# Block stores split over two DMA queues, a rotated order of the attention passes, and earlier slot preparation in a fused attention and mixture kernel

## What is computed

```python
q = x @ Wq + bq; k = x @ Wk + bk; v = x @ Wv + bv        # x layer-normed
k = k / jnp.maximum(jnp.linalg.norm(k, axis=-1, keepdims=True), 1e-12)
alpha, beta, gate = sigmoid(x @ Wa + ba), sigmoid(x @ Wb + bb), sigmoid(x @ Wg + bg)
def step(S, ins):
    trans = a_t[:, :, None] * (I - b_t[:, :, None] * kkT)
    S = jnp.einsum('bij,bjk->bik', S, trans) + b_t[:, :, None] * vkT
    return S, jnp.einsum('bc,bcd->bd', q_t, S) * g_t
x = x + (o @ Wo + bo)                                    # then, layer-normed again:
logits = jnp.einsum('bsd,etd->bset', xn, se)             # xn, se: RMS-normed x and slots
slots = jnp.einsum('bsd,bset->betd', xn, softmax(logits, axis=1))
processed = gelu(slots @ w1) @ w2
out = jnp.einsum('bnd,bsn->bsd', processed, softmax(logits over all slots))
x = x + out
```

## Time and profile before

| | us |
|---|---|
| median of 3 runs | 1261.44 |
| lowest and highest of them | 1257.5, 1261.8 |
| the profiled execution | 1255.7 |
| its span | 1254.0 |

### The profile page before, as it was taken

The page is one execution under the profiler, slowest core; times in us unless marked ns, Lnnn a source line. Parts: engine busy times, 40 slices in busy tenths (PEclk is TensorE's granted clock), DMA queues, the critical chain, the costliest instruction groups (busy, mean ns, idle before and its releaser), DMA issues.

```text
span 1254.0 us, 26991 instructions
## 1 busy us (share of the span) xinstructions
PE 1138.2 (91%) x8600; PEld 862.8 (69%) x8600; DVE 949.4 (76%) x2195; ACT 737.6 (59%) x1385; POOL 299.9 (24%) x373
## 2 busy tenths in 40 slices
PE   3588989898888977999999999999999999999998
PEld 2377767676677766568678568678468688477687
DVE  4568878788788884899757798656898666998655
ACT  3445555555555542578755478755477854487754
POOL 3345544555555541100002000002000012000012
PEclk9689999999999997999999999999999999999999
DMA  5112332223223313331327121337030346000045
GB/s 181 36 36 71 92 93 69 68 68 76 69 69 90 88 53 89 102 91 32 84 53 165 37 43 27 84 67 160 27 68 5 80 88 144 22 1 1 18 103 132
DMA packets 176941, 90.33 MB, mean 72 GB/s; under 512 B 117152, under 2 KB 170400, under 8 KB 176864
## 3 DMA queue, kind: packets, MB, share of 16 engines
q1 hardware_dynamic: 169808, 71.74, 24.5%
q0 software_dynamic: 5792, 17.05, 4.9%
q10 hardware_dynamic: 1264, 0.53, 0.2%
HBM read 38.42 MB, written 25.69 MB: 51 GB/s over the span
## 4 chain that ended last, share of the span: by engine, by line
PE 42%; DVE 23%; issue 10%; DMA 9%; ACT 6%; SPq 5%; DVEq 0%; POOL 0%; ACTq 0%; POOLq 0%
PE m_wide L1952 14%; DMA Mrep<-M_dram 8%; PE m_wide L1835 7%; PE m_wide L1929 5%; SPq L285 5%; PE m_wide L1915 4%; DVE m_Dm L1534 3%; DVE tmp L569 2%; PE m_wide L1940 2%; DVE Zc L580 2%; DVE m_El L1542 2%; DVE cmax L1505 2%; DVE rmax L1511 2%; ACT m_Eh L1717 2%; PE m_wide L1889 2%
## 5 line engine op out<-in xcount | busy, mean ns | idle before, releaser
L1472 POOL DMA_DIRECT2D out_dram<-m_o x64 | 35.5, 555 | 639.6 <-DVE m_o L1656 636.5
L1889 PE MATMUL m_wide<-m_X,m_Eh 128*128 128x257 f16 (+1 forms) x1024 | 171.1, 273 | 2.3 <-DVE m_El L1542 2.2
L1952 PE MATMUL m_wide<-m_Ph,m_Th 128*128 128x257 f16 x512 | 141.7, 277 | 10.5 <-DVE m_Pl L1581 10.5
L1835 PE MATMUL m_wide<-seT,XT 128*128 128x512 f16 x672 | 147.3, 379 | 0.1
L1952 PE MATMUL m_wide<-m_Ph,m_Tl 128*128 128x257 f16 x512 | 140.7, 275 | 0.0
L1952 PE MATMUL m_wide<-m_Pl,m_Th 128*128 128x257 f16 x512 | 140.4, 274 | 0.0
L1889 PE MATMUL m_wide<-m_X,m_El 128*128 128x257 f16 (+1 forms) x512 | 139.7, 273 | 0.0
L1835 PEld LDWEIGHTS m_wide<-seT,XT 128*128 (+1 forms) x672 | 65.5, 98 | 77.6 <-ACT L L1690 1.1
L1889 PEld LDWEIGHTS m_wide<-m_X,m_Eh 128*128 128x128 f16 x1024 | 99.2, 98 | 19.6 <-issue 3.5
L1690 ACT COPY L<-m_wide 128x512 f32<-128x512 f32 (+1 forms) x112 | 65.2, 585 | 77.0 <-PE m_wide L1835 76.2
L1753 ACT COPY m_Tl<-m_wide 128x1024 f16<-128x1024 f16 x64 | 64.7, 1011 | 75.5 <-PE m_wide L1940 75.5
(11 more groups left out here) (197 smaller groups left out, 2723.2 us busy)
## 6 DMA issues: line engine op xcount, KB each, us to landing
L<-in_L_attn_x_dram SPq DMA_DIRECT2D x16, 512.0 KB, 7.3
Mrep<-M_dram SPq DMA_DIRECT2D x16, 512.0 KB
x_dram<-x SPq DMA_DIRECT2D x16, 512.0 KB, 7.2
m_X<-X_dram SPq DMA_DIRECT2D x128, 64.0 KB, 1.8
m_x1t<-x_dram POOLq DMA_DIRECT2D x32, 256.0 KB, 3.5
out_dram<-m_o POOLq DMA_DIRECT2D x64, 128.0 KB, 2.5
X_dram<-Xh SPq DMA_DIRECT2D x16, 256.0 KB, 2.3
X_dram<-Xl SPq DMA_DIRECT2D x16, 256.0 KB, 2.3
```

The costliest lines, as they stand in the source:

```text
L1835: last = pe.matmul(lg[t % 4], XT[:, sx * KD + k, bass.ds((4 * g + t) * P, P)], seT[:, ss, k, z * HS:(z + 1) * HS], start=(c == 0), stop=(c ...
L1889: last = pe.matmul(acc[v][q], e[t % 4][:, qs], X[:, sx, bass.ds(4 * g + t, 1), 0:XW].rearrange("q a n -> q (a n)"), start=first and e is E ...
L1952: last = pe.matmul(co[p], a, pp[:, e, 0:XW], start=(c == 0), stop=(c == 3 * NS - 1))
```

## The change

What it does, in the attention:

- SP stores 4 of the 8 blocks (`range(NBK // 2)`), ACT the other 4, from its own queue, in a new `blocks_out` between `products(i+2, 0)` and `normalise(i+4)`.
- The read back is two DMAs, rows 0 to 7 of each block and then rows 8 to 15, each with a semaphore of its own. The base starts after the first; `product` 8 waits for the second.
- The border between two passes is moved on PE, ACT and DVE: `products` 2, `doubling` 2, `updates` and most `keys_values` now stand at the head of the next pass. On DVE `doubling` 2 comes after the first pair of the base, the first `biases` come before it, the others after pairs 6 and 7, `low_part` comes after all of `statistics`, and `moments` after `right_side`. On ACT `turned_x` 1 comes after `turned_Z` 1, `normalised` after `key_norms`, and `decayed` before `updates`. On POOL both `cut`, `residual` and the decayed queries change place.
- The slots are scaled and split in pass -1 instead of passes 12 and 13, turned on PE in pass 13 instead of 14, and the first four `early_logits` are made in pass 14. SP's first transposed load of X moves from pass 14 to pass 13.

In the mixture: `tp_ps` starts at 2 instead of 1, and ACT's waits on it are raised by one, so that only DVE's wait in `split_weights` is looser. ACT makes one tile of `weights` ahead of the first `processed_high` instead of two. The semaphore `going` is joined with `turning`.

```diff
             def blocks_out(c, q):
                 sp.wait_ge(M_ok, c + 1)
-                for e in range(NBK):
+                for e in range(NBK // 2):
...
-                sp.dma_start(Mrep[:, :, :, :].rearrange("p s b t -> p (s b t)"),
-                             M_dram.rearrange("e (a s) b t -> e a (s b t)", a=1).broadcast_to([NBK, BS, BS * B * BS]))\
-                    .then_inc(Mrep_in, 16)
+                for rows_in, s in ((Mrep_in, 0), (Mrep_late, HROWS)):
+                    sp.dma_start(Mrep[:, s:s + HROWS, :, :].rearrange("p s b t -> p (s b t)"),
+                                 M_dram[:, s:s + HROWS].rearrange("e (a s) b t -> e a (s b t)", a=1)
+                                 .broadcast_to([NBK, BS, HROWS * B * BS])).then_inc(rows_in, 16)
...
                     dve.wait_ge(col_ok, s)
+                    if s == HROWS:
+                        dve.wait_ge(Mrep_late, 16 * (c + 1))
...
+            def blocks_out(c, q):
+                act.wait_ge(M_ok, c + 1)
+                for e in range(NBK // 2, NBK):
+                    act.dma_start(M_dram[e],
+                                  M[q][e * BS:(e + 1) * BS, :, e * BS:(e + 1) * BS]).then_inc(M_out, 16)
...
                 def low_turned(k, t):
                     p, n = t % 2, b * HB + 2 * k + t // 2 + 1
-                    act.wait_ge(tp_ps[p], n + 1)
+                    act.wait_ge(tp_ps[p], n + 2)
...
-                for t in range(2):
-                    weights(0, t)
+                weights(0, 0)
                 for q in range(QS):
                     processed_high(0, q)
-                    if q < 2:
-                        weights(0, q + 2)
-                    elif q == 2:
+                    if q < QS - 1:
+                        weights(0, q + 1)
+                    if q == 2:
                         act.activation(table[:, 1:2], zero[:, :], ACT.Gelu)
...
-                pe.sem_inc(tp_ps[p], 1)
+                pe.sem_inc(tp_ps[p], 2)
```

More of the change, by code:

```diff
@@ L355, in step @@
                     store_x1(i)
+                if isinstance(i, int) and i == NCH - 3:
+                    blocks_landed(i + 2)
+                    sp.wait_ge(slots_ok, 1)
+                    load_XT0(0, XT0_PARTS[0])
                 if live(i + 4) and live(i + 2):
@@ L769, in step @@
                     next_state(i + 1, r, 3)
+                if live(i + 3):
+                    decays_from_start(i + 3, r, 0)
+                if live(i + 1):
+                    residual(i + 1, r)
+                if live(i + 2):
+                    doubling(i + 2, q, 0)
+                if live(i + 1):
+                    statistics(i + 1, 0)
+                if live(i + 3):
+                    decays_from_start(i + 3, r, 1)
+                if at == -2:
+                    mixture_weights(5)
+                if at == -1:
+                    slots_low()
+                if live(i + 4):
+                    turned_low(i + 4, 1)
+                if live(i + 1):
+                    statistics(i + 1, 1)
                 if at == NCH - 1:
@@ L958, in step @@
                 at = i if isinstance(i, int) else None
-                if at == NCH - 1:
-                    for t in range(4):
-                        early_logits_out(t)
-                if live(i):
-                    normalised(i)
+                if live(i + 1):
+                    turned_Z(i + 1, 2)
+                if live(i + 1):
+                    products(i + 1, 2)
+                if at == NCH - 2:
+                    turned_slots((6, 7))
+                if live(i + 1):
+                    turned_state(i + 1)
+                if live(i + 2) and live(i + 3):
+                    decayed(i + 2, q)
                 if live(i + 1):
@@ L973, in step @@
                     decay_and_step(i + 3, r)
+                if at == NCH - 1:
+                    for t in range(4, 8):
+                        early_logits_out(t)
+                if live(i):
+                    normalised(i)
+                if at == NCH - 2:
+                    early_logits_out(1)
+                    early_logits_out(2)
                 if live(i + 3):
                     queries(i + 3, r)
-                if live(i + 2) and live(i + 3):
-                    decayed(i + 2, q)
                 if live(i + 3):
@@ L1018, in _ @@
             steps(act, step)
-            for t in range(4, NT):
+            for t in range(8, NT):
                 early_logits_out(t)
@@ L1291, in _ @@
             steps(pe, step)
-            for t in range(NT):
+            for t in range(4, NT):
                 early_logits(t)
```

211 lines of the change are left out of this document (111 added, 100 removed).

## The result

The changed kernel takes 1263.22 us (median of 20 runs, 1257.26 to 1272.06), the kernel before 1257.41 (20 runs, 1246.76 to 1264.17). The ratio is 1.0052, 95% interval 1.0028 to 1.0076: slower by about half a percent, which is the border that the prediction drew. The profiled execution took 1258.68 us, 4.5 less than the median of its kernel; its span is 1256.9 against 1254.0 before.

A forecast was written before the change was run, and what follows sets the result against it. A ring of waits, no full engine, bounds the attention; PE nearly bounds the mixture. Terms +20, +1, -6.5, -9.8 make +4.7, rounded to +4: 1259.7 us profiled, 1265.5 median; 8-in-10 range 1249 to 1285.

The forecast's parts named there:

- The step from the profiled execution to the median: Profiled execution 1255.7 us against a median of 1261.44: 5.7 us difference, carried over to the changed kernel unchanged.
- The bounds of the half read: Attention, read back of the blocks' first half: 4.6 us expected, between 3.4 (bytes over all engines) and 5.6 (half the gain lost).
- The ring: Attention, chain of waits from one M to the next: 29.5 us per pass against 27.85, +20 us over 12 passes.
- The likeliest case: The forecast itself: half read holds up the base until +15.4, a pass of 29.5 us, 1265.5 us; chance 0.49.
- The start: Start of the attention, casts and slot work moved there: +1 us, with -2 and +4 as ends.
- the cover given to the slot work at the start: Attention's start: casts arrive before chunk 0's base, where DVE waited anyway; 3.25 us scaling and 1.7 us casting precede the next.
- The tail: End of the attention, slot work leaving the path: last three passes 6.5 us shorter, with -3 and -10 as ends.
- The mixture: Mixture, looser DVE wait 1.6 us and reordered `weights` 0.8 us per batch: -9.8 us, ends -6 and -11.
- The read is early enough: Attention: half read lands within 3.4 us, DVE itself bounds the base; pass of 28.2 us, 1250 in all; chance 0.22.
- Later still: Attention: `low_part` keeps 2.10 us as POOL runs late, half read takes 5.6; +23 us, 1288; chance 0.17.
- The two queues share the issue: Attention: ACT's four stores take 5 us, `normalise` and all behind start 2.5 us later; +30 us, 1296; chance 0.04.
- The mixture does not gain: Mixture: waits only change name, ACT's exponentials or last outputs come as late; +10 against the forecast, 1275; chance 0.08.

## Why the prediction was right in the end, and where it was not

The predicted 1265.5 us stand against 1263.22. That closeness is luck in good part: two terms were off by some 6.5 us each, with opposite signs. The step from the profiled execution to the median was off as well. I carried over 5.7 us, from three runs of the kernel before; its median of 20 runs is 1257.41, only 1.7 above the profiled execution, and for the changed kernel the step is 4.5. So the medians differ by 5.8 us where the forecast had 4. Two slips in the sum are small: 22.7 and 6.9 make 29.6 and not 29.5 us (1.2 us over 12 passes), and four times 2.4 is 9.6 and not 9.8. The bounds of the half read do not follow from their words either: a quarter of 5.6 us above 1.8 gives 3.2, and half of the gain lost gives 6.0, where 3.4 and 5.6 stand.

**The ring, mechanism right, size too large.** The likeliest case was what happened. Its steps against the means of the twelve passes: `low_part` done at +10.2 (9.8 measured), read issued at +10.8 (10.8), first half 4.6 us (4.6), base at +15.4 (15.4), updates at +16.3 (16.3). Only the last two terms were mis-sized: from the updates to the heads 6.4 us, taken from before, took 5.9 in 11 of 12 passes (6.0 in the mean), and from there to M 6.7 instead of 6.9. That makes the 0.5 us per pass between 29.5 and 28.98. The steps are right as means, but not in each pass: in five of the twelve PE's clock fell behind the pause at `turn_x`, the DVE work behind it came later, and DVE waited for the read only 0.0, 0.2, 0.6, 0.9 and 1.5 us there, against 1.2 to 1.7 in the others. I had priced that pause at its length alone, and its clock only as a part of a rival. Part of it returns in other executions: the profile of the version with DVE's wait of the mixture put back has the same attention code and a ring of 29.79, because PE's clock fell there between the updates and the heads in 6 of 12 passes, against 1. The median of the changed kernel, 4.5 us above its profiled execution, fits that, but I have no trace of a median run.

**The start, wrong.** I counted +1 with +4 as the upper end; it was +7.6. The step that failed is the cover given to the slot work at the start, "arrive later in front of the base of chunk 0 where DVE waited anyway" and the 3.25 and 1.7 us ahead of the next base. I counted them as work against a wait of DVE, and did not follow that in the new order `doubling` 2, and so the updates, stand behind them. Against before M(2) - M(1) grew by 4.6 us (35.2 from 30.6), and with the slots late it was 28.6. The second piece is ACT's stores: M(1) - M(0) is 31.8 us with them, 29.6 before, and 27.9 in the version with all stores on SP, since PE's `turn_x` of the next chunk, which waits for `normalise`, starts 4.8 us behind M(0) with them and 0.9 in that version. This holds for the rotated order only: in the order of before the split made this stretch shorter, 26.5 us. The third stays open: M(0) is 1.8 us later (30.25 from 28.45). It lies at 27.6 to 28.5 in four profiles of the old order and at 30.2 to 31.9 in nine of the rotated one, but at 28.1 in a tenth, so whether the order or the first loads make it I can't tell. M(3) - M(2) is 1.0 us shorter, and with that the pieces make the 7.6.

**The tail, right within 1 us.** -5.5 against -6.5. What ends last there are DVE's maxima, 1.2 us per tile, one behind the other in both profiles but for one `low_part`: from the first early one to the mixture's first it is 21.3 us before and 20.6 after. So 4.9 of the 5.5 us are won ahead of them. That the four early logits gained nothing by themselves fits this, but no run tests it. The slot work is tested: with it back in pass 12, the way from M of chunk 15 to the first early maximum grows by 2.5 and 3.5 us.

**The mixture, right, a little too small.** -12.8 against -9.8, and outside its end of -11: DVE's wait was worth 2.1 us per batch instead of 1.6, the order of the exponentials, by subtraction, 1.1 to 1.3 instead of 0.8. PE's wait ahead of `combine` fell as said, to about 1 us per batch:

```profile
PE m_wide L2006 <- DVE m_Pl L1636: 4.2, 4, 1.1
```

**The rivals.** "The read is early enough" did not happen: DVE waited in 11 of the 12 passes. "Later still" neither: POOL was idle and `low_part` took 1.21 us; but its other half, PE's clock falling in the pauses at `turn_x`, did happen in five of the twelve passes, and these take 28.5 to 30.0 us. "The two queues share the issue" is refuted: four stores take 2.54 us on SP and 2.5 to 2.9 on ACT, side by side, against 5.07 and 5.14 for eight on one in the rows shown. "The mixture does not gain" is refuted by both runs on it.

**What I had not seen** is that the harm has two links, and that they are not both the split's. One is the wait of SP behind Xl. It comes from the new place of `low_part`, stays without the split, and is worth 1.4 to 1.9 us per pass with the split in place (27.54 and 27.12 against 28.98) and 2.4 without it (25.42 against 27.78). The other is ACT's four stores ahead of `normalise`: with the read still behind Xl they cost 1.2 us per pass (28.98 against 27.78), with the read ahead of it 2.1 (27.54 against 25.42), since PE stands still at `turn_x`. I had the second only as a link to the first. Either way the two make 3.6 us.

Part of the second link is PE's clock. Two windows of the changed kernel, each from `turn_x` on, behind a pause of 1.68 and of 1.67 us:

```profile
217.30:223.30 6.00, 5.82 (x37) 5.62 (x38) 2.62 (x5) 1.83 (x5) 3.23 (x3) 0.72 0.02 7
332.50:338.50 6.00, 5.88 (x50) 5.32 (x50) 4.03 (x13) 2.14 (x5) 3.19 (x3) 1.00 0.05 15
```

PE gets through 37 matmuls in the first and 50 in the second. Such a fall at `turn_x` stands in five of the twelve passes of the changed kernel, in three with the read ahead, in one with `low_part` moved back and in five of the kernel before with the split. It stands in none of the versions with all stores on SP, where the pause is gone.

## What to carry to other kernels

Before a DMA is moved to a second queue, look at what that engine does next. Here 2.5 us of issue were taken off SP, where they cost nothing once the read came in halves (with eight stores on SP and a read that need not wait for Xl, DVE waits at most 0.15 us for the blocks, in either order of the passes), and put ahead of `normalise`, on which PE, DVE and the next M depend. When work is moved later on one engine, look at who waits for its result: `low_part` was not on the path before. And SP issues in the order of its program: a read that everything waits for must not stand behind a store whose data come late. One exchanged pair of lines was worth 24 us by the medians (1263.22 to 1239.65), 17 by the profiled executions. When several small terms make up a sum, check each against the trace by itself, since a good total can hide two bad terms.

## What the runs showed of the hardware

**The same pause costs more or less, by the clock.** Two passes of the changed kernel: the updates of the one follow an idle time of 1.75 us, those of the other one of 1.39 us. Windows from about the updates on:

```profile
343.50:350.90 7.40, 7.18 (x44) 6.12 (x45) 5.96 (x27) 4.21 (x15) 1.61 (x3) 0.77 0.30 106
372.50:378.60 6.10, 5.05 (x39) 4.23 (x40) 5.30 (x26) 2.49 (x12) 0.00 (x0) 1.00 0.46 157
```

The first ran with part of its matmuls at the lower of the two levels (1.2 against 2.4 GHz), a mean granted clock of 0.77, and took 7.3 us to the heads; the second 5.9. The length of the pause alone does not decide it: in the changed kernel a pause of 1.72 us at the same place was followed by 5.9 us too, and in the version with all stores on SP one of 2.52 us by 5.9 and one of 2.33 us by 7.3. With the whole read the pauses of 3.9 to 5.2 us were each followed by slower matmuls, with 0.67 in the window shown, and 7.1 to 8.5 us to the heads. So a pause of PE ahead of the critical matmuls costs its own length and up to 2.6 us more, and not in every pass.

**DVE against POOL, whoever is first.** `low_part` took 2.10 us in the kernel before, from 313.15 to 315.25, where POOL had begun an operation 0.3 us earlier:

```profile
312.87 1.29 POOL L436 TENSOR_TENSOR L<-M_,a_const 128x512 f32<-128x512 f32 x1
314.13 2.25 POOL L431 TENSOR_TENSOR qTg_<-qT_,gbc_ 128x512 f32<-128x512 f32 x1
```

The first POOL operation keeps its 1.29 us and DVE is late; the second one, begun while DVE was at work, takes 2.25 us, where it takes 1.27 in the changed kernel. In the version with `low_part` moved back, DVE began first:

```profile
342.50 1.22 DVE L670 TENSOR_TENSOR Xl<-xf,Xh 128x1024 f16<-128x1024 f32 x1
```

```profile
342.52 3.58 POOL L445 TENSOR_TENSOR L<-M_,a_const 128x512 f32<-128x512 f32 x2
```

Now DVE has its 1.22 us, and POOL's two cuts take 3.58 us instead of 2.54 in the changed kernel. The delay, 0.9 to 1.0 us, falls on the one that starts second. The Trainium skill ("SBUF — State Buffer", section "Who interferes with whom") says that the order of issue, and not the shape of the operation, decides who is held up. The trace agrees: DVE takes 2.10 us as the second and 1.22 as the first. My 2.0 us for that place, taken from before, was therefore wrong.
